# Token tiles from the last unit of the fifth step on, residual sums on VectorE, six row groups, first gathers waited for one by one

## The reference

```python
x = layernorm(x + attn(x))       # a gated convolution with a scan, its own layernorm
x = layernorm(x + xattn(x, ctx)) # 3 iterations over "slots" = the 4 x 1024 tokens
x = layernorm(x + ffn(x))
# xattn, one iteration:
sn = rmsnorm(slots); scores = (sn @ Wq.T) . k * D**-0.5
attn = softmax(scores over the slots axis = -2); attn = attn / (attn.sum(-1) + eps)
slots = gru_cell(attn @ v, slots)      # r, z = sigmoid(...); n = tanh(xn + r * hn)
                                       # slots = (1 - z) * n + z * slots
# ffn: 8 experts, top 1
chosen = argmax(x @ gate_w.T); y = x + expert_w[chosen] @ x
```

## Time and profile before

| | us |
|---|---|
| median of 3 runs (lowest, highest) | 714.59 (713.61, 715.01) |
| profiled execution, its own time | 714.96 |
| span of its trace | 713.0 |

### The profile page before, as it was taken

The page is one execution under the profiler, slowest core; times in us unless marked ns, Lnnn a source line. Parts: engine busy times, 40 slices in busy tenths (PEclk is TensorE's granted clock), DMA queues, the critical chain, the costliest instruction groups (busy, mean ns, idle before and its releaser), DMA issues.

```text
span 713.0 us, 7225 instructions
## 1 busy us (share of the span) xinstructions
PE 548.4 (77%) x2136; PEld 406.4 (57%) x2136; DVE 453.3 (64%) x768; ACT 394.5 (55%) x650; POOL 331.4 (46%) x247
## 2 busy tenths in 40 slices
PE   5956766344765599989989989998998998309981
PEld 2433424233533388768867867876887877306661
DVE  0588987676532455995895797598375767624551
ACT  2716268264863366746846666674575663404662
POOL 0373524633323014563464446456235366743674
PEclk9988889656795799999999999999999999658997
DMA  8200303042110000000000000000110061224541
GB/s 300 66 0 1 118 0 108 11 160 105 59 60 1 0 1 1 0 0 1 1 0 1 0 1 0 1 0 1 60 59 31 30 214 38 97 97 139 176 143 42
DMA packets 23286, 37.87 MB, mean 53 GB/s; under 512 B 3149, under 2 KB 15054, under 8 KB 22992
## 3 DMA queue, kind: packets, MB, share of 16 engines
q1 hardware_dynamic: 19840, 28.98, 12.6%
q0 software_dynamic: 3408, 8.43, 3.3%
HBM read 23.60 MB, written 14.72 MB: 54 GB/s over the span
## 4 chain that ended last, share of the span: by engine, by line
PE 33%; DVE 16%; issue 11%; POOL 4%; ACT 3%; DMA 1%; SPq 0%; POOLq 0%; DVEq 0%; ACTq 0%
PE psum L950 22%; PE psum L875 5%; POOL out L1293 3%; DVE slots_full L1433 3%; DVE gru L1431 2%; PE psum L917 2%; DVE gru L1413 2%; DVE at L1404 2%; DVE sc L1395 1%; DVE at L1406 1%; PE psum L863 1%; DVE ss_part L1371 1%; POOL sorted_rows L1285 1%; ACT sc L1076 1%; PE psum L994 1%
## 5 line engine op out<-in xcount | busy, mean ns | idle before, releaser
L950 PE MATMUL psum<-slots_hi,w_hh 128*128 128x512 f32 x576 | 189.1, 410 | 12.0 <-DVE gru L1413 12.0
L1256 POOL TENSOR_TENSOR gru<-slots_full,gru 128x512 f32<-128x512 f32 x48 | 74.4, 1551 | 176.8 <-ACT gru L1098 176.8
L950 PEld LDWEIGHTS psum<-slots_hi,w_hh 128*128 128x128 f32 x576 | 110.0, 194 | 38.3 <-DVE gru L1413 13.7
L950 PE MATMUL psum<-slots_lo,w_hh 128*128 128x512 f32 x288 | 117.0, 406 | 0.0
L950 PE MATMUL psum<-at,v_ih 128*128 128x512 f32 x288 | 93.9, 408 | 1.4 <-DVE at L1406 1.4
L471 PE MATMUL psum<-x_fm,w_in 128*128 128x512 f32 x128 | 63.7, 660 | 19.9 <-ACT g L282 12.3
L1413 DVE SCALAR_TENSOR_TENSOR gru<-psum,vec,gru 128x512 f32<-128x512 f32 x48 | 35.9, 748 | 51.1 <-PE psum L950 46.3
L1098 ACT ACTIVATE gru<-gru,vec 128x512 f32<-128x512 f32 x48 | 34.7, 723 | 57.1 <-DVE gru L1420 56.7
L950 PEld LDWEIGHTS psum<-slots_lo,w_hh 128*128 128x128 f32 x288 | 56.0, 195 | 14.0
L950 PEld LDWEIGHTS psum<-at,v_ih 128*128 128x128 f32 x288 | 54.8, 194 | 15.9 <-DVE at L1406 3.6
L471 PEld LDWEIGHTS psum<-x_fm,w_in 128*128 128x128 f32 x128 | 27.0, 214 | 54.6 <-issue 33.0
(11 more groups left out here) (192 smaller groups left out, 1100.0 us busy)
## 6 DMA issues: line engine op xcount, KB each, us to landing
gathered<-sorted_rows SPq DMA_DIRECT2D x39, 129.0 KB, 2.1
x_fm<-in_xT SPq DMA_DIRECT2D x4, 1024.0 KB, 6.6
x_tm<-in_x SPq DMA_DIRECT2D x4, 1024.0 KB, 7.1
x_scratch<-slots_full SPq DMA_DIRECT2D x8, 512.0 KB, 3.0
x_block<-x_scratch SPq DMA_DIRECT2D x8, 512.0 KB, 3.9
slots_full<-in_expertT SPq DMA_DIRECT2D x1, 2048.0 KB, 10.2
sorted_rows<-gru SPq DMA_DIRECT2D x1, 1032.0 KB, 12.1
whh_raw<-in_whhT SPq DMA_DIRECT2D x1, 768.0 KB, 8.5
```

The lines of the kernel that those rows point to most:

```text
L950: last = pe.matmul(psum[:, bank, :], w, d, start=start and i == 0, stop=stop and i == len(pairs) - 1)
L1256: pool.tensor_tensor(DF(u), full[:, c, seq(k, h), blk(j)], X(u), ALU.subtract).then_inc(d_pool, 1)
```

## The change

- The tiles begin in (4,7): tiles 0 to 2 in its slots, tile 3 behind it, 4 to 7 in and behind (5,0), and so on; `BANK_OF`, `BEFORE` and the ranks' places are new, and so is where each row stands on ScalarE and each score on VectorE.
- `gate_mean` and `gate_centre` move to step 0: behind XN of (0,2) on TensorE, behind `settle(0, 1)` on VectorE; the scores of step 1 wait for it.
- `add_x1(3)` to `add_x1(6)` move from GpSimd to VectorE (semaphore `w_mid`), each behind a `settle`.
- The groups are 8, 8, 4, 4, 4, 4; GpSimd sends 1, 4, 4, 4, 4, 4 rows behind differences 1 to 6 and 11 behind the last.
- `add_ident(0)` moves behind `tile_table`. `token_scores` now lies over the constants of the mean squares and sums, whose last use is in (4,5), and no longer over buffers that step 4 still needs.
- SyncE loads the first three row numbers before it waits for the sends, and the first three gathers have a semaphore each, on which `turn` waits one by one.

```diff
-        GROUPS = ((0, NT), (NT, NT), (2 * NT, NT), (3 * NT, TJ), (3 * NT + TJ, TJ))
+        GROUPS = ((0, NT), (NT, NT), (2 * NT, TJ), (2 * NT + TJ, TJ), (3 * NT, TJ), (3 * NT + TJ, TJ))
+        BANK_OF = (6, 7, 6, 7, 6, 7, 6, 7, 7, 6, 7, 6, 7, 6, 7, 6, 6, 7, 6, 7, 7, 6, 7, 6, 6, 7, 6, 7, 0, 1, 2, 5)
+        BEFORE = (None, None, 0, 1, 2, 3, 4, 5, 7, None, 8, 9, 10, 11, 12, 13, 15, None, 16, 17, 19, None, 20, 21,
+                  23, None, 24, 25, None, None, None, None)
+        DEST_BEFORE = {9: 1, 17: 3, 21: 5, 25: 7}
+        RANK_B = (6, 7, 6, 7, 4, 6)
+        RANK_BEFORE = (7, 15, 19, 23, None, 27)
 ...
 # SyncE
+                first_rows = [row_of(i) for i in range(TG)]
                 for g, (_, n) in enumerate(GROUPS):
                     sp.wait_ge(row_out[g], 16 * n)
-                for g in range(NG):
+                for i in range(TG):
+                    sp.dma_start(gat[:, i, :], rows[bass.ds(first_rows[i], P), :]).then_inc(gat_first[i], 16)
+                for g in range(1, NG):
 ...
 # TensorE
                 def scores(f):
+                    if f == 1:
+                        pe.wait_ge(g_set, 1)
 ...
                 def gate_mean():
                     pe.wait_ge(gw_in, 16)
-                    pe.wait_ge(d_ln, PAIRS)
+                    pe.wait_ge(ss_ln, 2)
 ...
+                    unit(k, 2, {"R": lambda: mean_squares(k + 1, 3), "XN": lambda: None if k else gate_mean()})
 ...
+                unit(LAST - 1, 7, {"R": tile(0), "HN": tile(1), "XN": tile(2)})
                 token_tile(3)
+                unit(LAST, 0, {"R": tile(4), "HN": tile(5), "XN": tile(6)})
                 token_tile(7)
+                unit(LAST, 1, {"HN": lambda: ranks(0), "XN": tile(8)})
+                token_tile(9)
+                token_tile(10)
+                unit(LAST, 2, {"R": tile(11), "HN": tile(12), "XN": tile(13)})
                 token_tile(14)
+                unit(LAST, 3, {"R": tile(15), "HN": lambda: ranks(1), "XN": tile(16)})
+                token_tile(17)
+                unit(LAST, 4, {"R": tile(18), "HN": tile(19)})
+                unit(LAST, 5, {"R": lambda: ranks(2), "HN": tile(20), "XN": tile(21)})
+                token_tile(22)
+                unit(LAST, 6, {"R": tile(23)})
+                unit(LAST, 7, {"R": lambda: ranks(3), "HN": tile(24), "XN": tile(25)})
+                for n in range(26, 4 * NT):
                     token_tile(n)
                 ranks(4)
+                ranks(5)
 ...
 # ScalarE: in (4,7) r_gate, row(0), row_square(0), n_gate, row(1), z_gate, row_square(1), row(2), row_square(2)
                 for q, (first, second, third, fourth) in enumerate((
-                        (0, 1, 2, 3), (4, 5, 6, 7), (8, 9, 10, None), (11, 12, 13, 14), (15, 16, 17, None),
-                        (18, 19, None, 20), (21, 22, 23, None), (None, None, 24, None))):
+                        (3, 4, 5, 6), (7, None, 8, None), (9, 10, 11, 12), (13, 14, 15, 16),
+                        (17, 18, None, 19), (None, None, None, 20), (21, 22, 23, None), (None, None, None, 24))):
 ...
 # GpSimd
+                for q, n in ((1, 1), (2, 4), (3, 4), (4, 4), (5, 4), (6, 4), (7, 11)):
+                    difference(LAST, q)
+                    for i in range(sent, sent + n):
+                        send_row(i, group_of[i])
+                    sent = sent + n
 ...
 # VectorE, its order from (4,7) on, as it now stands (h: hidden_part, i: input_part, s: settle):
 # h(4,7) score 0, i(4,7) score 1, s(4,6) score 2, h(5,0) score 3 4, i(5,0) s(4,7) add_x1(3) score 5 6 7 choose 0,
 # h(5,1) side 0 destinations 0, i(5,1) s(5,0) score 8 9, h(5,2) score 10 11, i(5,2) s(5,1) add_x1(4)
 # score 12 13 14 15 choose 1, h(5,3) destinations 1, i(5,3) s(5,2) side 1 score 16 17, h(5,4) score 18, i(5,4)
 # s(5,3) add_x1(5) score 19 choose 2, h(5,5) destinations 2, i(5,5) s(5,4) side 2 score 20 21 22, h(5,6)
 # score 23, i(5,6) s(5,5) add_x1(6) choose 3, h(5,7) side 3 destinations 3, i(5,7) s(5,6) add_last(0)
 # score 24 25, s(5,7) add_last(1) score 26 27 choose 4, score 28 to 31 choose 5, side and destinations 4, 5,
 # tile_table, add_ident(0), add_ident(1)
```

More of the change, by code:

```diff
@@ L85, in decoder_layer @@
         ident = sb("ident", [P, P])
+        over_means = ExitStack()
+        scs = space(over_means)("token_scores", [P, B * NT, NS])
+        over_means.close()
         mean_h = [sb(f"mean_half{h}", [P, P], F32R) for h in range(2)]
@@ L1037, in _ @@
-                unit(LAST, 7, {"HN": lambda: ranks(2), "XN": lambda: token_tile(24)})
-                for n in range(25, 4 * NT):
+                unit(LAST, 3, {"R": tile(15), "HN": lambda: ranks(1), "XN": tile(16)})
[5 more added lines that the diff above has]
+                unit(LAST, 7, {"R": lambda: ranks(3), "HN": tile(24), "XN": tile(25)})
@@ L1039, in _ @@
+                for n in range(26, 4 * NT):
                     token_tile(n)
-                    if n == 27:
-                        ranks(3)
                 ranks(4)
+                ranks(5)
                 pe.wait_ge(z_act, UL + QU)
-                pe.matmul(psum[:, CNT_B, 0:E], ones_f[:], cum(4)[:, :, TJ], start=True, stop=True).then_inc(cnt_mm, 1)
+                pe.matmul(psum[:, CNT_B, 0:E], ones_f[:], cum(5)[:, :, TJ], start=True, stop=True).then_inc(cnt_mm, 1)
                 pe.wait_ge(more_set, 1)
@@ L1217, in _ @@
                         row(first)
-                        row(second)
+                        if second is not None:
+                            row(second)
                         row_square(first)
@@ L1601, in _ @@
                     settle(k, 1)
+                    if k == 0:
+                        gate_centre()
                     tops(k + 1)
@@ L1616, in _ @@
                     attention(k + 1)
[L1617 to L1618 removed]
                     if later:
+                        candidate(k, 7)
+                        settle(k, 6)
                         ss_low(k + 2, 2)
[L1621 removed]
+                hidden_part(LAST - 1, 7)
                 score(0)
+                input_part(LAST - 1, 7)
+                score(1)
+                settle(LAST - 1, 6)
+                score(2)
                 hidden_part(LAST, 0)
[L1624 to L1627 removed]
                 score(3)
                 score(4)
[L1630 removed]
+                input_part(LAST, 0)
+                settle(LAST - 1, 7)
+                add_x1(3)
                 score(5)
[L1632 to L1633 removed]
                 score(6)
@@ L1636, in _ @@
                 choose(0)
+                hidden_part(LAST, 1)
+                side(0)
+                destinations(0)
+                input_part(LAST, 1)
+                settle(LAST, 0)
                 score(8)
+                score(9)
                 hidden_part(LAST, 2)
-                score(9)
+                score(10)
+                score(11)
                 input_part(LAST, 2)
                 settle(LAST, 1)
-                score(10)
-                side(0)
-                destinations(0)
-                score(11)
-                hidden_part(LAST, 3)
+                add_x1(4)
                 score(12)
-                input_part(LAST, 3)
-                settle(LAST, 2)
                 score(13)
```

179 lines of the change are left out of this document (83 added, 96 removed).

## The result

| | before | after |
|---|---|---|
| median, us (lowest, highest) | 714.1 (709.41, 715.01) | 735.01 (731.29, 736.54) |
| profiled execution, its own time | 714.96 | 736.54 |
| span of its trace | 713.0 | 734.8 |

The change makes the kernel slower: ratio 1.0313, 95% interval 1.0274 to 1.0352. The forecast of 734.0, slower, was right; for the profiled execution it had +19.0, and the trace has +21.8.

The account below looks back on a forecast made before the run. TensorE bounds the last step, then GpSimd's row sends. Later scores +1.7, later last send +20.6 and earlier gathers -3.3 sum to +19.0: 734 us, range 722 to 744 by the clock, 720 to 745 with other bounds.

Parts of the forecast that it names:

- (a): Gate mean in step 0: its centring makes the scores of step 1 start later, +1.7 us.
- (b): From (4,7) on, TensorE waits for late rows, scores and choices: 3.7 us ahead of tile 2, 23.3 after.
- (c): Clock from tile 2 to ranks 3: seven gaps over 1.8 us each cost 1.7, 11.9 us in all.
- (d): Four adds moved to VectorE: 1.23 us each, delay inside the tile gaps; GpSimd possibly held up 4.9 us in all.
- (e): Tail with six groups and more sends ahead: 18.8 us from last unit's end to last send, not 27.9; -9.1.
- (f): First gathers after the sends: row addresses loaded ahead of the wait make turn(0) start earlier, -3.3 us.
- The clock holds: Rival for the last step: the short gaps bring no low clock, so 722 us; chance 0.16.
- The clock falls more often: Rival for the last step: every gap from 1.1 us up drops the clock, six more at 1.7, 744; chance 0.14.
- Not slower: Rival for twelve places where tiles wait: rows come in time, 30.0 us less, 704; chance 0.07.
- Gathers bring 1.0: Rival for the first gathers: they save only the register load, 1.0 us, so 736; no chance of its own given.

Follow-up runs that it names:

- e1: The change with only VectorE's and ScalarE's lists reordered, so each tile's score and row precede its bank's next use; ratio 0.992 to the kernel before.
- e9: e1 with the gate mean moved ahead of step 0 and GpSimd's last difference one send earlier; ratio 0.9874 to the kernel before.
- e3: The change with the gate mean and its centring moved ahead of step 0; ratio 1.0278 to the kernel before.
- e7: The change with matmuls nobody reads in TensorE's gaps ahead of tiles 2, 7, 13, 16 and ranks 2, 3; ratio 1.0245 to the kernel before.
- e2: The change with two scores on VectorE each put ahead of the hidden part they stood behind; ratio 1.0216 to the kernel before.
- e6: The kernel before with only the change's edit to the first gathers; ratio 0.9965 to the kernel before.
- e4: The change with the four sums moved back from VectorE to GpSimd; ratio 1.0306 to the kernel before.
- e5: The change with the first three gathers again each behind its own register load and waited for as a group; ratio 1.0361 to the kernel before.
- c0: The change run again without edits, on another chip; ratio 1.0312 to the kernel before.
- e10: e9 with the fifth group's destinations ahead of the sixth's choice and only one row number loaded ahead; ratio 0.9852 to the kernel before.

## Why the prediction was right

The mechanism is the one forecast; that the median came within 1.0 us of 734 is partly luck. Along the trace the sum was 2.8 us short, and this is what is left of errors of both signs: +1.0 behind (a), some +3.6 in (b), -1.7 to -3.3 in (c).

- **What bounds the kernel.** TensorE in the last step, then GpSimd's sends. e1 and e9 confirm both: with the gaps gone, all that is left after the unit's end counts one for one.
- **(a)** +1.7, measured +1.6 at the scores; e3 takes it back. Its effect downstream, 2.65 to 3.0, was not foreseen: the sum took everything later to shift by 1.7, and two longer stretches of low clock came with it (e3).
- **(b)** The gaps came where they were put, 27.9 of 27.0 us, and end with the rows and sums that were named. They are a matter of list order alone: e1 takes them away with the same instructions. The term that was too small is the round trip. The 59.7 us of work take 0.234 for every matmul, also for the last one ahead of a gap. But the last HN matmul of (5,0) starts at 550.75 and takes 0.40, and the hidden part starts at 551.25, 0.50 behind that start. Over 16 gaps the last matmul's 0.40 makes some 2.7 us, and the gap lengths have 0.9 more: 3.6. (The 0.66 of a hidden part is not the step of the earlier trace rows, which is 0.79 to the next operation; behind the hidden part of (5,0) the score starts 0.67 later.)
- **(c)** Seven drops at 1.7 were predicted. Five came: tile 22's gap was 1.60 and not 1.9, and ranks 2's 2.38 us brought none; one was twice as long. 8.6 by e7 instead of 11.9. That a gap over 1.8 us brings a drop, taken from two rows, is refuted: 2.46 us did in the change and did not in e2, 2.73 did in the change and did not in e3, 1.82 did in the kernel before and did not in e6. The gap just ahead does not decide it either: in e3 it is tile 5's 1.59 as in the change, and in e6 there is none, as in the kernel before. What does is open. A drop's cost is no constant: 1.7 or 3.4. This error runs against that of (b): by the windows' 10.2 the two come to +1.9 of the 2.3 us by which this stretch was underestimated (32.0 from the start of (4,7), predicted 29.7), by e7's 8.6 only to +0.3. Which is nearer is open, since e7's fillers change the gaps a little too.
- **(d)** The port block that the Trainium skill, "SBUF — State Buffer", section on the two separate sides, describes showed itself in the direction that the sum had, the add waiting (2.10 instead of 1.23); the other direction, up to 4.9 us of GpSimd waiting, does not show at any of the four sums: the difference was first each time and ran 1.60 to 1.63. The four adds take 3.5 us more than at 1.23 each. e4: 0.2 us for all four sums.
- **(e)** 18.4 from the unit's end to the last send, predicted 18.8. The parts are not as predicted, and that they add up is luck: the first of the last eight sends starts 8.8 after the unit's end and not 9.9, since the tail tiles run at clock 1.00 (20 matmuls in 2.84), while tile 26 and ranks 5 wait 1.64 and 1.50; and the seven steps to the last send take 9.5 and not 8.9.
- **(f)** Predicted -3.3, with turn(0) 4.7 after the last send; measured 5.09 and, by e5, -2.9.
- **The rivals.** "The clock holds" was priced at 722; e7 holds it up to the last unit's end and still loses 2.5% (731.6). "The clock falls more often" wanted 13 drops; five came. "Not slower" was priced at 30 us for twelve places where rows come late; e1, which keeps the first of them (tile 2, with its drop) and clears ranks 2 and 3 besides, gives 33.0 at the last unit's end and 27.8 at turn(0). Its condition, another list order, is not in this change. "Gathers bring 1.0" is refuted by e5.

## What to carry to other kernels

When a block of work is moved to an earlier slot, write down for each slot which in-order engine must have passed which instruction before the buffer is free; a producer placed behind an operation that itself waits for the engine you want to feed costs a full round trip (1.2 to 2.7 us here), and reordering two lists is worth more than the move. Count a low-clock stretch (1.7 us here, at times 3.4) as a risk of each gap of some 2 us, not as a rule, and price a round trip from the last matmul's own row, not from the pitch of a full pipeline. After the last compute unit, look which queue the last small operation stands in. And when two traces of nearly the same kernel part by a microsecond, look for the place before explaining it by the edit: here it was one pair of operations, 0.05 us apart, that had changed places.

## What the runs showed of the hardware

- The last stage, a steady stream of gathers, transposes and scatters, takes 71 to 72 us on the first chip and 84 to 87 on the two others, in all kernels, while the places ahead of it agree within 0.1 us for the change (after and c0).
- The granted clock after equal gaps differs: 2.46 us ahead of tile 13 gives 0.53 over the next 3 us in the change and 1.00 in e2; 2.73 ahead of tile 7 gives 0.62 in the change and 1.00 in e3; 1.82 ahead of the first tile gives 0.75 over 6.85 us in the kernel before and 1.00 in e6.
- Which of a VectorE and a GpSimd operation of 128x512 starts first, by 0.05 us, decides which of them is the long one: 0.69 and 1.79 in e9, 1.79 and 1.29 in e10. TensorE's first tile moved by 1.3 us with it.
- Three register loads in a row on SyncE took 3.9 us in e6, in a stretch in which VectorE stalled too; in e5 three loads with the issue of two gathers between them took 3.3.
